# Batch 5's slot sums, a gate's half sum and tile 30's statistics in another order behind the last tile

## The reference, cut to what matters

```
x = x + tanh([context(align(layernorm(x))), layernorm(x)] @ W_c.T)
xn = layernorm(x)
h = gelu([xn, slot_mean] @ w1 + b1);  logits = (h @ w2 + b2) / (|tau| + 0.1)
alpha = softmax over the 8 largest of 64 logits, scattered back, for each row
si = einsum('bts,btd->bsd', alpha, xn) / (alpha.sum(t) + 1e-8)
gi = si @ Wih.T + bih;  gh = S @ Whh.T + bhh       # 3 gates: r, z, n
S_new = (1 - z) * n + z * S;  then attention among the 64 slots, layernorm, @ wvp
x = x + einsum('bts,bsd->btd', alpha, slot_values) @ wo + bo
```

## Time and profile before

| | us |
|---|---|
| median of 3 runs | 343.57 |
| lowest, highest | 343.3, 344.89 |
| the profiled execution | 343.45 |
| its span, first to last instruction | 341.6 |
| PE busy | 327.2 (96%) |
| DVE busy | 250.0 (73%) |
| POOL busy | 205.9 (60%) |
| ACT busy | 201.8 (59%) |

### The profile page before, as it was taken

The page is one execution under the profiler, slowest core; times in us unless marked ns, Lnnn a source line. Parts: engine busy times, 40 slices in busy tenths (PEclk is TensorE's granted clock), DMA queues, the critical chain, the costliest instruction groups (busy, mean ns, idle before and its releaser), DMA issues.

```text
span 341.6 us, 7115 instructions
## 1 busy us (share of the span) xinstructions
PE 327.2 (96%) x2316; PEld 282.8 (83%) x2316; DVE 250.0 (73%) x751; ACT 201.8 (59%) x408; POOL 205.9 (60%) x350
## 2 busy tenths in 40 slices
PE   8999999999999999999999999989999999999970
PEld 6688768998998989989989989977789877777750
DVE  5799887766785877877877777757935674678872
ACT  3485264659569578776778678576753355223430
POOL 5001459787877886785776767636683337046772
PEclk9999999999999999999999999999999999999996
DMA  7999967423242332322423100019600000000897
GB/s 279 310 321 384 326 175 216 121 67 123 63 122 66 91 97 64 123 64 63 124 64 97 59 2 2 0 16 356 225 3 0 2 0 0 0 2 1 340 368 277
DMA packets 40950, 42.79 MB, mean 125 GB/s; under 512 B 3261, under 2 KB 32061, under 8 KB 40914
## 3 DMA queue, kind: packets, MB, share of 16 engines
q1 hardware_dynamic: 38960, 40.19, 36.0%
q10 hardware_dynamic: 1666, 1.49, 1.4%
q0 software_dynamic: 288, 0.66, 0.7%
HBM read 32.18 MB, written 8.39 MB: 119 GB/s over the span
## 4 chain that ended last, share of the span: by engine, by line
PE 75%; POOL 9%; issue 7%; ACT 5%; DVE 2%; POOLq 0%; ACTq 0%; DVEq 0%
PE psum L465 17%; PE psum L466 16%; PE psum L467 16%; PE psum L1775 4%; PE psum L2040 3%; POOL hT_lo L610 3%; PE psum L1806 3%; PE psum L1604 2%; PE psum L1755 2%; PE psum L1843 2%; ACT th L1335 1%; POOL r2all L621 1%; PE psum L1577 1%; PE psum L1664 1%; PE psum L1989 1%
## 5 line engine op out<-in xcount | busy, mean ns | idle before, releaser
L465 PE MATMUL psum<-GW_hi,hT_hi 128*128 128x292 f32 (+1 forms) x256 | 78.7, 307 | 0.1
L467 PE MATMUL psum<-GW_lo,hT_hi 128*128 128x292 f32 (+1 forms) x256 | 73.9, 289 | 0.0
L466 PE MATMUL psum<-GW_hi,hT_lo 128*128 128x292 f32 (+1 forms) x256 | 73.9, 289 | 0.0
L615 POOL TENSOR_TENSOR X<-X,th 128x512 f32<-128x512 f32 x32 | 38.7, 1210 | 28.1 <-ACT th L1335 28.1
L465 PEld LDWEIGHTS psum<-GW_hi,hT_hi 128*128 128x128 f32 x256 | 48.4, 189 | 1.5 <-issue 1.1
L466 PEld LDWEIGHTS psum<-GW_hi,hT_lo 128*128 128x128 f32 x256 | 48.3, 189 | 0.1
L467 PEld LDWEIGHTS psum<-GW_lo,hT_hi 128*128 128x128 f32 x256 | 48.1, 188 | 0.0
L982 DVE BATCH_NORM_STATS2 st<-X 128x6 f32<-128x512 f32 x32 | 22.2, 693 | 25.2 <-POOL X L615 25.2
L610 POOL TENSOR_TENSOR hT_lo<-xT,hT_hi 128x512 fp32r<-128x512 f32 x30 | 39.2, 1306 | 2.0 <-DVE stack L993 2.0
L465 PE MATMUL psum<-xhT_hi,w_hi 128*128 128x256 f32 x128 | 37.8, 296 | 0.8 <-issue 0.5
L466 PE MATMUL psum<-xhT_hi,w_lo 128*128 128x256 f32 x128 | 36.1, 282 | 0.0
(11 more groups left out here) (319 smaller groups left out, 905.4 us busy)
## 6 DMA issues: line engine op xcount, KB each, us to landing
xT<-in_xT SPq DMA_DIRECT2D x32, 256.0 KB, 2.7
X<-in_x SPq DMA_DIRECT2D x32, 256.0 KB, 3.5
out<-ost SPq DMA_DIRECT2D x32, 256.0 KB, 3.0
WhhT<-in_WhhT SPq DMA_DIRECT2D x1, 3072.0 KB, 13.6
WihT<-in_WihT SPq DMA_DIRECT2D x4, 768.0 KB, 8.0
Wo<-in_wo ACTq DMA_DIRECT2D x4, 256.0 KB, 4.4
WvpT<-in_WvpT SPq DMA_DIRECT2D x4, 256.0 KB, 5.1
WaT<-in_WaT SPq DMA_DIRECT2D x1, 1024.0 KB, 11.4
```

What stands on the lines that cost most here:

```text
L465: pe.matmul(out, w_hi, m_hi, start=start, stop=False)
L466: pe.matmul(out, w_lo, m_hi, start=False, stop=False)
L467: return pe.matmul(out, w_hi, m_lo, start=False, stop=stop)
L615: pool.tensor_tensor(tile_x(r), tile_x(r), halves(th[:, :]), ALU.add).then_inc(S("x2"), 1)
```

## The change

Four lists are put in another order; the operations and their number stay. On POOL the root and scale of tile 30 come ahead of the residual of tile 31. On DVE, in step 31, the last part of batch 5's top-k comes ahead of batch 4's slot inputs (it came behind them), tile 30's statistics close the step instead of following `low_xh(29)`, and `low_slot_sums(4)` comes ahead of tile 31's statistics instead of behind them; a wait for ag2 that stands there stays. On ACT `norm2(31)` comes ahead of `logits_biased(6)`. On PE batch 5's slot sums are done one tile before `context(31)` and three before `first_layer(32)`, instead of all four behind `logits(6)`; `turn_slots(5)`, `first_layer(33)` and `turn_rows(31)` come ahead of `turn_logits(6)`; the first gate's half sum comes between first layers 33 and 34; and batch 6's first two tiles of slot sums come ahead of `logits(7)`, its other two ahead of `turn_logits(7)`.

```diff
--- before.py
+++ after.py
@@ -652,8 +652,8 @@
         pool.wait_ge(S("hl"), 2)
         for s in range(NT):
             step(s)
+        scales2(30)
         residual(31)
-        scales2(30)
         scales2(31)
 
 
@@ -1055,13 +1055,16 @@
             if s in TOPK_STEP:
                 logits_out(TOPK_STEP.index(s))
             extras(s)
+            if s == NT - 1:
+                topk(5, 2)
+                slot_inputs(4)
             for b in range(NB):
                 for part in range(3):
-                    if TOPK_STEP[b] + part == s:
+                    if TOPK_STEP[b] + part == s and s < NT - 1:
                         topk(b, part)
-                if SLOT_STEP[b] + TPB - 1 == s:
+                if SLOT_STEP[b] + TPB - 1 == s and s < NT - 1:
                     slot_inputs(b)
-            if live(s - 1) and s < NT - 1:
+            if live(s - 1):
                 stats2(s - 1)
             if s in ROW_STEP:
                 offset_row(ROW_STEP.index(s))
@@ -1071,10 +1074,9 @@
 
 
         low_xh(29)
-        stats2(30)
+        low_slot_sums(4, TURN)
         v.wait_ge(S("ag2"), NT - 1)
         stats2(31)
-        low_slot_sums(4, TURN)
         slot_inputs(5)
         high_piece_of(0)
         high_piece_of(1)
@@ -1430,8 +1432,8 @@
         gelu(6, 1)
         turned_slots(4, TURN)
         norm2(30)
+        norm2(31)
         logits_biased(6)
-        norm2(31)
         high_xh(30)
         high_xh(31)
         turned_slots(5, TURN)
@@ -1883,27 +1885,30 @@
             step(s)
 
         turn_weights(31)
+        slot_sums(5, 0, 1)
         context(31)
         pe.wait_ge(S("th"), NT - 1)
         turn_slots(4, TURN)
+        slot_sums(5, 1, TPB)
         first_layer(32, 0)
         first_layer(32, 1)
         logits(6)
-        slot_sums(5)
         turn_rows(30, 4, 2)
+        turn_slots(5, TURN)
+        first_layer(33, 0)
+        first_layer(33, 1)
+        turn_rows(31, 4, 2)
         turn_logits(6)
-        turn_slots(5, TURN)
-        turn_rows(31, 4, 2)
-        for s in (33, 34, 35):
+        gate_sum(0, 0, 0, HN)
+        for s in (34, 35):
             first_layer(s, 0)
             first_layer(s, 1)
 
-        gate_sum(0, 0, 0, HN)
         turn_alpha(5, trX, 0)
+        slot_sums(6, 0, 2)
         logits(7)
-        slot_sums(6, 0, 2)
+        slot_sums(6, 2, TPB)
         turn_logits(7)
-        slot_sums(6, 2, TPB)
         gate_sum(0, 2, 0, HN)
 
         pe.wait_ge(S("te"), EP)
```

## The result

The changed kernel takes 344.15 us (median of 13 runs, 343.66 to 345.21), the kernel before in the same comparison 343.48 (13 runs). The ratio is 1.0024 with a 95% interval of 1.0013 to 1.0035: slower by 0.8 us, 0.45 to 1.2, inside the half per cent that was given 0.86. The profiled execution has a span of 342.3 us.

The account below looks back on a forecast made before the run. PE was taken to bound the kernel, without slack against DVE; 1.14 us of closed holes return as 0.4 + 0.3 + 0.9, so 343.45 + 0.4 = 343.85, taken as 343.9 us; range 342.3 to 345.2.

Parts of the forecast that it names:

- The holes named in PE's timeline: PE idle 1.14 us from 227.20 to 241.24, including 0.35 before `context(31)`, 0.53 before `first_layer(32)`, 0.24 before `turn_slots(5)`; these close.
- A2 of batch 5, the statistics, the roots: DVE and POOL around step 31: A2 at 225.75, tile 31's statistics at 231.4, normalisation starting 232.8 instead of 233.54.
- The allowance of 0.45: 0.45 us allowed for two-SBUF-input products in DVE's moved top-k, running while POOL adds tile 30's residual.
- PE's sum up to `turn_logits(6)`: PE's new queue from 227.33, summed step by step: `turn_logits(6)` ends at 235.33 instead of about 234.15.
- The switch price: On PE, 0.20 us extra where a first-layer step follows slot sums.
- rival 2: WihT's first quarter lands too late, DVE waits before the first W rounding; slower, up to 345.5; chance 0.07.
- DVE's chain shifts as one block: DVE's work from `logits_out(6)` to batch 6's sin, 12.21 us back to back, all ends 0.47 later.
- rival 3: POOL takes the port before a second of DVE's four roundings: block 1.08 us longer, time 345.0; chance 0.07.
- The three meetings: PE waits for late DVE before `first_layer(34)`, `slot_sums(6, 0, 2)` and `turn_slots(6)`: holes of 0.4, 0.3 and 0.9 us.
- Rival 1: PE's own queue sets the end, holes stay closed: faster, 342.2 to 343.2 us; chance 0.27.
- The slack I named: At `turn_rows(31)` on PE, input ready since 233.6: 0.9 us to spare, hiding the costs on DVE and POOL.

Follow-up runs that it names:

- e2: Changed kernel with `low_xh(30)` ahead of `logits_out(6)` on DVE; ratio to the kernel before 1.0002, stretch 37.52 us.
- e3: Changed kernel with gate (0, 1)'s half sum ahead of `turn_slots(6)` on PE; ratio to the kernel before 1.0013, stretch 37.92 us.
- e4: Changed kernel with three gate half sums brought forward on PE between slot transposes and sums; ratio to the kernel before 0.9977, stretch 36.75 us.
- e6: Changed kernel with the edits of e2 and e4 together; ratio to the kernel before 0.9971, repeated 0.9954; stretch 36.21 us.
- e8: Changed kernel with the reordering on POOL and DVE around tiles 30 and 31 undone; ratio to the kernel before 1.0035, stretch 38.58 us.
- e5: Changed kernel with batch 5's slot sums in one piece behind `turn_slots(4)`; ratio to the kernel before 1.0022, stretch 38.32 us.

## Why the prediction was right, point by point

**The holes named in PE's timeline close.** Shown: none is left at its place.

**A2 of batch 5, the statistics, the roots.** Predicted times of the new order, set from `turn_weights(31)`, held within 0.11 us: A2 ended at rel -1.31 (predicted -1.29), `residual(31)` started at 2.10 (2.16), tile 31's aggregation ended at 4.29 (4.36), its normalisation started at 5.65 (5.76). The allowance of 0.45 for the top-k part beside POOL's residual was needed: the small product took 0.67, and ended 0.01 us after POOL's addition, 226.22 and 226.21 (rows above). By the rule of the Trainium skill, page "SBUF — State Buffer", section "SBUF: two separate sides", an operation with two SBUF inputs waits for the whole of GpSimd's; this row agrees. The price as such was off the path, as said: A2 was there 1.5 us before PE's first tile of sums (rel 0.20).

**PE's sum up to `turn_logits(6)`.** The term that failed: "the context costs 0.24 ... ended at 228.04", with the first tile of sums at 0.47. The chain of waits of the changed kernel has 0.59 and 0.44 for them:

```profile
228.27 0.59 PE psum L1777 x4
228.85 0.44 PE psum L1845 x2
229.29 0.22 PE psum L1792 x2
229.51 1.46 PE psum L1777 x12
```

That is 0.32 more, plus 0.04 on the other three tiles, where 0.13 was allowed. The switch price I had put on `first_layer` behind slot sums (0.20) is also due where the context follows them. Two consequences: the copy of the logits came 0.66 late and not 0.47, and the weight loads were issued at rel 1.32 instead of 1.16, where I had them unmoved. On the clock of the kernel before the copy started at 235.57, just past the 235.3 to 235.5 that I had named as a sign. The first quarter of WihT was there 5.1 us after its issue (229.32 to 234.46), with 1.3 us to spare before the copy of the logits could start: rival 2 did not come. The quarter did touch PE at another place. POOL makes the first low piece of W behind it, and the weight load of `gate_sum(0, 0)` waited for that:

```profile
236.41 0.19 PEld L465 LDWEIGHTS psum<-siT_hi,W_hi 128*128 128x128 f32 x1 [0.17 <-POOL W_lo L666]
```

**DVE's chain shifts as one block.** Shown. Predicted 12.21 us from the copy to the end of sin; it took 12.13 (236.53 to 248.66), with the same 3.59 for four roundings, so rival 3 did not come either. e2 shows that the block sets PE's end: `low_xh(31)`, and all of the block behind it, came 0.53 earlier and the stretch was 0.53 shorter.

**The three meetings.** Predicted holes 0.4, 0.3 and 0.9; the profile has 0.15, 0.35 and 1.09. The first is released by "issue", which names no engine, but PE starts 0.10 behind the end of `low_xh(31)`, 238.25 and 238.15. It is short only because `gate_sum(0, 0)` ahead of it began 0.17 late for the low piece of W; in e3 and e4, where that piece was there in time, it is 0.34. `turn_slots(6)` was predicted 0.38 later and came 0.48 later, `slot_sums(7)` 0.38 and came 0.55. The shift then goes through to the gates unchanged (0.55 at the first wide matmul).

**Size.** Forecast +0.4 us; the stretch shows +0.55, the timing +0.8 (0.45 to 1.2) and, once more, +0.3 (-0.1 to 0.6). So the forecast lies just below the first interval and inside the second: the timing can't test a size this small, the stretch can. The term that was too small is the switching of the split. What the first timing has above 0.55 is within the scatter.

**Rival 1, PE's own queue sets the end**, fell with e3 in its simple form, since filling one hole only moved it. What it would take came out in e4 and e6: work on PE between each of DVE's results and its user.

Of the order of the statistics the prediction counts the costs, and rightly calls them hidden; that its gain is on the path I missed until e8, which shows 0.53 us. In the prediction this did no harm, because the sum went through the kernel that has it: `slot_inputs(5)` was placed right, at 232.3, with its user at 232.9. The slack I named, 0.9 us at `turn_rows(31)`, was not the smallest: my own times leave 0.6 at `turn_slots(5)` (232.3 to 232.9).

Left open: whether anything outside the stretch differs between the two kernels by some tenths; the profiles' heads and tails scatter by over 1 us, too much to tell.

## What to carry to other kernels

When idle time of the busiest engine is closed by a new order, follow each thing it now does later to the in-order queue that waits for it, and count all that stands behind the waiting instruction. Here a copy waiting 1.31 us held 12 us of DVE's work that came back to PE as three holes; one swap on DVE gave nearly all of it back, and with spare gate sums between DVE's results and their users as well the stretch became 1.3 us shorter than before. Look for the smallest slack among all that stands behind a moved operation, not only at the one the edit is about.

## What the runs showed of the hardware

A stretch of 37.5 us deep in the kernel repeats within 0.02 us from execution to execution, on the same program, while in two executions of the kernel before its start lay 1.6 us apart (227.04 and 228.63) and the tail behind it 0.6 (77.06 and 76.45). For edits of some tenths of a microsecond the distance between two instructions in one profile each told more than the timing, whose intervals were 0.1 to 0.2% to either side. Where a group of matmuls of one kind stood behind another kind, its first steps were dearer: four passes of slot sums took 0.59 us behind a transpose, where a quarter of 16 in one piece is 0.47, and the two matmuls of a context 0.44 behind slot sums, where the chain of waits has 0.24 for them behind matmuls of the scores (223.98, the context of tile 30). That the change of kind is the cause is my reading; no run here varied it alone. e5 shows what the split is worth with it: it saves a wait of 0.36 and gains 0.27 net. Behind a wait of 1.09 two transposes moved the chain by 0.44 us, without one by 0.22.
